# Cross-attention with the fourth head block's maxima, peak row, subtraction and exponential moved beside the next batch's first scores

## What is computed

```python
def _L0_xattn_ref(x, y, Wq, Wk, Wv, Wp, bp):
    q = _split_heads(x @ Wq)
    k = _split_heads(y @ Wk)
    v = _split_heads(y @ Wv)
    attn = jnp.einsum('bhid,bhjd->bhij', q, k) * SCALE
    attn = jax.nn.softmax(attn, axis=-1)
    out = jnp.einsum('bhij,bhjd->bhid', attn, v)
    ...
    return out @ Wp + bp
x = x + _L0_xattn_ref(_layernorm(x, axis=-1), ctx_1024, ...)
```

## Time and profile before

| | |
|---|---|
| median of 3 runs | 1876.14 us (1875.85 to 1878.16) |
| the profiled execution: time | 1876.37 us |
| its span in the profile | 1874.3 us |
| TensorE busy | 1834.6 us (98%) |
| VectorE busy | 1123.5 us (60%) |
| ScalarE busy | 835.4 us (45%) |
| GpSimd busy | 884.5 us (47%) |
| mean granted TensorE clock | 0.997 of full speed |

### The profile page before, as it was taken

One profiled execution on the slowest core, in us unless ns is written; L12 is line 12 of the kernel. 1 busy time (PEld: TensorE's weight loads), 2 busy tenths in 40 slices (PEclk: granted clock), 3 DMA queues, 4 the chain that ended last, 5 costly groups with the idle time before them and its releaser, 6 DMA issues. The chain is left out here.

```text
span 1874.3 us, 65622 instructions
## 1 busy us (share of the span) xinstructions
PE 1834.6 (98%) x29024; PEld 1590.0 (85%) x29024; DVE 1123.5 (60%) x1368; ACT 835.4 (45%) x1033; POOL 884.5 (47%) x830
## 2 busy tenths in 40 slices
PE   7999999999999999999999999999999989999998
PEld 6989898989888888888888888888888867777887
DVE  5666575757474747484848484838384747572265
ACT  4545454545454545353535353535353523343322
POOL 0374545454555545454646363637373753344111
PEclk9999999999999999999999999999999999999999
DMA  6100111111010202020202020202020231122110
GB/s 247 56 4 21 61 30 51 43 38 54 27 64 17 71 10 78 3 79 2 79 2 78 2 78 2 79 2 78 2 78 2 70 117 59 25 91 90 45 57 23
DMA packets 40812, 94.54 MB, mean 50 GB/s; under 512 B 18784, under 2 KB 20320, under 8 KB 40544
## 3 DMA queue, kind: packets, MB, share of 16 engines
q1 hardware_dynamic: 40544, 90.26, 13.6%
HBM read 81.99 MB, written 6.16 MB: 47 GB/s over the span
## 5 line engine op out<-in xcount | busy, mean ns | idle before, releaser
L487 POOL TENSOR_TENSOR fold<-fold,prob 128x256 f32<-128x256 f32 (+1 forms) x704 | 705.7, 1002 | 55.2
L98 PE MATMUL ring<-y_parts,w_keep 128*128 128x402 f32 (+1 forms) x3072 | 607.5, 351 | 1.4 <-PEq L174 1.4
L98 PE MATMUL ring<-wv_s,y_parts 128*128 128x512 f32 (+1 forms) x2496 | 596.5, 396 | 0.0
L98 PEld LDWEIGHTS ring<-y_parts,w_keep 128*128 128x128 f32 x3072 | 551.1, 188 | 17.1 <-issue 3.9
L98 PEld LDWEIGHTS ring<-wv_s,y_parts 128*128 128x128 f32 (+1 forms) x2496 | 453.7, 184 | 112.6
L481 POOL TENSOR_TENSOR fold<-prob 128x256 f32<-128x256 f32 x64 | 68.3, 1067 | 686.7 <-ACT prob L524 686.7
L501 ACT ACTIVATE k_sb<-ring 128x402 f32<-128x402 f32 (+1 forms) x256 | 129.4, 506 | 370.9 <-PE ring L98 370.9
L647 DVE TENSOR_TENSOR prob<-prob,peak_rows 128x1024 f32<-128x1024 f32 (+1 forms) x192 | 277.9, 1499 | 12.1 <-ACT peak_rows L520 12.1
L514 ACT ACTIVATE prob<-s_ps 128x1536 f32<-128x1536 f32 (+1 forms) x128 | 199.9, 1562 | 128.8 <-PE s_ps L774 128.8
L524 ACT ACTIVATE prob<-prob 128x1024 f32<-128x1024 f32 (+1 forms) x192 | 207.5, 1123 | 2.9 <-DVE prob L647 1.0
L774 PEld LDWEIGHTS s_ps<-q_sb,k_sb 32*64 32x64 f32 x13312 | 156.3, 130 | 28.5 <-issue 28.5
(11 more groups left out here) (196 smaller groups left out, 1494.7 us busy)
## 6 DMA issues: line engine op xcount, KB each, us to landing
y_raw<-yT SPq DMA_DIRECT2D x48, 804.0 KB, 7.2
y_raw<-yT SPq DMA_DIRECT2D x16, 792.0 KB, 10.0
f_raw<-w_ffn SPq DMA_DIRECT2D x22, 512.0 KB, 3.2
p_x<-x SPq DMA_DIRECT2D x4, 512.0 KB, 6.5
q_scratch<-p_x SPq DMA_DIRECT2D x8, 256.0 KB, 2.0
q_sb<-q_scratch SPq DMA_DIRECT2D x16, 128.0 KB, 8.2
x_sb<-x SPq DMA_DIRECT2D x4, 512.0 KB, 6.7
aw_raw<-y_raw SPq DMA_DIRECT2D x8, 256.0 KB, 3.5
```

What stands on the lines that cost most here:

```text
L98: mm = pe.matmul(out, left(a, c), right(b, c), start=(c == 0 and n == 0), stop=(c == DC - 1 and n == 2))
L487: pool.tensor_tensor(acc[0:m], acc[0:m], prob[0:m, i, t, :], ALU.add).then_inc(sum_step, 1)
```

## The change

The turn of block 3 leaves the values phase of its batch, except in the last batch, and stands in the next batch's keys of block 1. On TensorE `turn(b - 1, 3)` stands ahead of `scores(b, 0, 0)` and `spread_peaks(b - 1, 3)` ahead of `scores(b, 0, 1)`. On VectorE `peaks(b - 1, 3)` stands ahead of `largest(b, 0, 0)`, and `subtract(b - 1, 3)` between `largest(b, 0, 0)` and `output(b - 1, 1)`. On ScalarE the peak row and the three exponentials stand between the key chunks of block 1. GpSimd's code is the same.

```diff
@@ keys_phase on ScalarE
                 for i in range(1, NBLK):
+                    of = (b, i - 2) if i >= 2 else (b - 1, NBLK - 1)
                     key(b, i, 0)
                     score(b, i - 1, 0)
                     key(b, i, 1)
-                    if i >= 2:
-                        peak_row(b, i - 2)
+                    if past or i >= 2:
+                        peak_row(*of)
                     score(b, i - 1, 1)
                     key(b, i, 2)
-                    if i >= 2:
-                        exponential(b, i - 2, 0)
-                        exponential(b, i - 2, 1)
+                    if past or i >= 2:
+                        exponential(*of, 0)
+                        exponential(*of, 1)
                     key(b, i, 3)
-                    if i >= 2:
-                        exponential(b, i - 2, 2)
+                    if past or i >= 2:
+                        exponential(*of, 2)
@@ values_phase on ScalarE
                 value(b, 5)
-                peak_row(b, 3)
                 if more:
                     high(b + 1, 1)
                 else:
+                    peak_row(b, 3)
                     gather(0)
                 value(b, 7)
-                exponential(b, 3, 0)
-                exponential(b, 3, 1)
-                exponential(b, 3, 2)
+                if not more:
+                    exponential(b, 3, 0)
+                    exponential(b, 3, 1)
+                    exponential(b, 3, 2)
@@ keys_phase on VectorE
+                if past:
+                    peaks(b - 1, 3)
                 largest(b, 0, 0)
                 if past:
+                    subtract(b - 1, 3)
                     output(b - 1, 1)
                 largest(b, 0, 1)
@@ values_phase on VectorE
-                peaks(b, 3)
+                if not more:
+                    peaks(b, 3)
                 value(b, 6)
-                subtract(b, 3)
+                if not more:
+                    subtract(b, 3)
@@ batch on TensorE
                 if past:
-                    small_rows(b - 1, 3)
+                    small_rows(b - 1, 2)
                     weigh(b - 1, 0)
                 keys(b, 0, 2)
                 keys(b, 0, 3)
                 keys(b, 1, 0)
+                if past:
+                    small_output(b - 1, 0)
+                    turn(b - 1, 3)
                 scores(b, 0, 0)
                 keys(b, 1, 1)
+                if past:
+                    spread_peaks(b - 1, 3)
                 scores(b, 0, 1)
                 keys(b, 1, 2)
                 if past:
-                    small_output(b - 1, 0)
+                    small_rows(b - 1, 3)
                     weigh(b - 1, 1)
                 keys(b, 1, 3)
...
-                small_rows(b, 2)
-                turn(b, 3)
+                if not more:
+                    small_rows(b, 2)
+                    turn(b, 3)
                 values(b, 6)
-                spread_peaks(b, 3)
+                if not more:
+                    spread_peaks(b, 3)
```

More of the change, by code:

```diff
@@ L813, in weigh, with batch @@
                 mm.then_inc(pv_ok, 1)
-            def batch(b, past):
+            def batch(b, past, more=True):
                 keys(b, 0, 0)
@@ L873, in _ @@
                 batch(b, True)
-            batch(B - 1, True)
+            batch(B - 1, True, False)
             small_rows(B - 1, 3)
```

## The result

The changed kernel takes 1914.83 us (median of 4 runs, 1912.51 to 1916.97) against 1875.99 us before: ratio 1.0203, 95% interval 1.0191 to 1.0216. It is 38.8 us slower, about 10 us more than the forecast of 29. One of the four runs, 1916.97 us, lies outside the range of 1888 to 1916. The profiled execution took 1913.74 us, with a span of 1911.7 us, 37.4 more than before.

A forecast was written before the change was run, and what follows sets the result against it. TensorE, busy 98% of the span, was taken as the bound. New waits of 27.6 us plus 2.6 for the moved transposes and spread, less batch 0's 1.0, gave +29.2 us: 1905.5 us, 1.6% slower, range 1888 to 1916.

The forecast's parts named there:

- the first wait: TensorE's transposes of block 0 wait for VectorE's last maximum, 1.84 us in each of batches 1 to 15: +27.6 us.
- the moved pair: Block 3's transposes and spread on TensorE cost 0.50 us at the new place, 0.17 more than before: +2.6 us over 15 batches.
- the second wait: Rival: block 1's transposes also wait, 0.3 to 1.0 us; at 0.5 it adds 7.5 us, giving 1913; chance 0.23.
- Nothing to gain in the values phase: TensorE never waits there for the maxima in the fifteen later batches, only 1.0 us once in batch 0; moving softmax frees nothing.
- batch 0's 1.0 to 1.2 us: TensorE's single wait of the transposes for the maxima, in batch 0's cross-attention, goes with its transposes: -1.0 us.
- The subtractions are covered: Block 3's moved subtractions on VectorE end before the second output can start, with 1.2 us to spare.
- GpSimd starts a microsecond before the maxima and stretches them to 5.27 us: GpSimd's moved totals start at 704.12, VectorE's five block 0 maxima at 705.10; these take 5.27 instead of 3.05 us.
- No second wait in the likeliest case: Block 1's transposes have 1.15 us of room against 1.1 of delay; a wait at block 0 alone has chance 0.57.
- The rival of a whole GpSimd add for each maximum: Each of block 0's five maxima stands behind one 0.99 us GpSimd add, taking 8.0 us: +41, 1946 us; chance 0.03.

## Why the prediction came out as it did

The sign and the main mechanism held, and the range did too, though near its upper end and in part by luck: errors of opposite sign met in the sum. The forecast of +29.2 us is about 10 short of the measured 38.8. In the profiled execution, what was changed makes +34.7 us (the last three rows of the table), 5.5 above the forecast. Against this the sum holds 3.4 us too much for the first wait and 2.6 too much for the moved pair, and leaves out 6.6 for the second wait in 12 batches, 4.8 for the three with a slow stretch (1.6 each beyond the first wait) and 1.2 for block 2's transposes, which come 0.1 us later in the 12. That is 6.6 us in all, against 5.5. The other 2.7 us of that execution lie ahead of the change.

- *Nothing to gain in the values phase.* Right. With the new waits out of the way the kernel is 0.1% faster than before, and batch 0's 1.0 to 1.2 us suffice for that.
- *The moved pair, +0.17 us a batch.* Wrong in size: zero. After the change the step from three key chunks to the scores grows from 6.79 to 7.01 us and the one to the second scores from 3.59 to 3.79, 0.42 together, not 0.50; and the eleven value tiles without the pair take 0.41 us less, not 0.33. The two cancel. This took 2.6 us too much into the sum.
- *The subtractions are covered.* Right: 1.17 us to spare, forecast 1.2.
- *GpSimd starts a microsecond before the maxima and stretches them to 5.27 us.* Right: 0.98 us before, 5.14 us. That this makes the wait is shown from both sides, by taking the additions away and by adding some to the kernel before. The wait was 1.6 and not 1.84 us a batch: the maxima are 0.13 shorter, and the way from the last maximum to the matmul took 0.06 and not 0.14 us.
- *No second wait in the likeliest case.* This is the step that failed. The rival came true, with 0.55 us, and it should have been the likelier: the room of 1.15 us was reckoned to the end of the maxima. But block 1's transposes also wait for `output(b - 1, 2)` (`small_output`), which VectorE does behind these maxima, so the room was 0.42 us, as the run with two extra maxima shows. In the changed kernel both the maxima of block 1 and the output end 0.97 us later, counted from block 0's transposes (13.79 against 12.82 and 14.52 against 13.55). Of 1.15 us of room this would have left some; of 0.42 it leaves 0.55 too little, the measured wait. The rival's own working priced the delay at 1.1 us, so its cost was about right and the room was the error. At 12 of 15 batches the wait is worth 6.6 us.
- *The clock.* Left out altogether. Behind waits of 1.6 us and more the granted clock fell to its lower level in some batches; each of the three in the profiled execution is 0.9 us longer than a batch with both waits. The other executions of the changed kernel have mean clocks of 0.989 to 0.994 and times of 1912.5 to 1917.0, the slower ones at the lower clock, so this share varies from run to run.
- *The rival of a whole GpSimd add for each maximum.* Refuted by the 5.14 us that the maxima take, against its 8.0, and by its time: its +41 us stand on top of the forecast, so it gives 1946 us, 31 above the measured. Beside GpSimd a 512-column maximum takes 1.11 us, 0.42 more than alone, while GpSimd's additions take 0.73 us alone. The Trainium skill, page "SBUF — State Buffer", section "SBUF: two separate sides", has the lock held for a whole instruction. The traces agree that the two engines slow each other, and not that the loser waits for a whole instruction.

What stays open: why the first of the five maxima runs at full speed in one kernel beside GpSimd and not in another, and why some batches get the lower clock and others not.

## What to carry to other kernels

When a step moves, follow the work on other engines that it releases: here every moved instruction fitted its new place, and what set the time was an engine whose code was not touched, adding sums beside maxima that had 0.4 us of room. Reckon room from everything that the waiting instruction waits for, the buffer's last reader included, not from its data alone. Here swapping two instructions within the crowded stretch moved the wait to the next place and made it no cheaper. Whether a place with more room beside it would have been free was not tried.

## What the runs showed of the hardware

- Sharing with GpSimd cost VectorE's two-input maxima the same time whatever their width: beside the real totals (0.73 us alone) 512 columns took 1.11 us instead of 0.69 and 256 columns 0.84 instead of 0.42, both 0.42 more; beside additions of a tile to itself (0.61 us alone) they took 0.98 and 0.72, both 0.3 more.
- A 256-column maximum whose semaphore had long been reached, right behind another, ran in 0.41 us beside GpSimd, whose addition took 1.14 instead; the next, which waited for it, took 0.85.
- TensorE's granted clock fell to its lower level behind single waits of 1.6 to 3.4 us in a stream that was otherwise full: in 3 of 14 batches with waits of 1.6 and 0.55 us, 4 of 14 with one of 1.6, 11 of 14 with one of 1.75, all 14 with one of 3.4, and in none with one of 0.8 to 1.3 us or without a wait. A batch with a wait of 1.75 us and such a stretch was up to 1.6 us longer than one with the wait alone.
